# Two streams of TensorE products alternated in the half tiles of a mixture of experts, and a step of VectorE's order moved in the attention in front of it

## The chip, the cores and the metric

One Trainium2 (trn2) chip, one of its cores. The metric is the device time of one execution in microseconds (us).
## The reference, cut to what matters

One layer on x of 8 x 512 tokens with 256 features:

```python
qkv = x @ w_qkv.T                      # 16 heads of 16
q, k = rope(rms_norm(q, qw), rms_norm(k, kw))
x = layernorm(x + (softmax(causal(q @ k.T / 4)) @ v) @ w_proj.T)
normed = x * rsqrt(mean(x * x) + 1e-8) * norm_weight
shared = relu(normed @ sw1 + sb1) @ sw2 + sb2          # 256 -> 1024 -> 256
w, idx = top_2(sigmoid(normed @ router_w.T))           # of 8 experts, weights normalised
routed = sum over the two of w * (relu(normed @ ew1[e] + eb1[e]) @ ew2[e] + eb2[e])
out = layernorm(x + shared + routed)
```

The kernel keeps fp32 accuracy by splitting each operand into a high and a low fp16 half and adding three products (high x high, high x low, low x high).

## The kernel before

**Front stage.** The attention of the eight blocks c (512 tokens each), the routing, and the scatter of token rows to the experts are one software pipeline. All engines go through positions g = -33 to 209; `due(offsets, g)` lists the jobs of a kind at a position: block c does a job with offset o at g = 20c + o. So a block takes 20 positions, and several blocks are in work at once. At one position an engine does its kinds of jobs in a fixed order that its `step(g)` spells out. What this case touches, by position within a block (modulo 20):

- Position 18: TensorE transposes the last query and key rows of block c + 2 (`TR`, L1511 for the queries, L1517 for the keys). ScalarE copies the query columns (L886), VectorE the key columns (L1301), both into `stk`. TensorE's first score product of the next block (`UNITS`, p = 0, L1470, position 0) waits for both copies.
- Position 18 too: `added(c, 1)` on VectorE (L1111 to L1123) adds the projection to x and takes mean and variance; GpSimd's `norms` (L648 to L658) and `shifted` (L678) follow at position 19 from its result `vv`.
- Positions 17 and 1: `normalised(c, 0)` and `normalised(c, 1)` on VectorE, for the pairs of row tiles 0 and 1 of block c: two products `xnf` (L1133), the high half (L1136) and the low half (L1137) of the token rows `xnh`. They wait for GpSimd's `x1_done`. Their readers are TensorE's transposes at offsets 42 and 48 (positions 2 and 8) and GpSimd's scatters from offset 58 on.
- Positions 0 to 8, VectorE: normalised queries and keys (`qn`), GpSimd's copies of them (L631, L638, L639) and its half of the rotation (L619, L622), `averaged` at positions 4, 6, 8 and 10 (L1092, L1093; output `an`), which frees the bank `mb` that TensorE's L1622 fills.
- At some positions VectorE also makes the low half of a chunk of expert weights (L1335); at position 17 this comes behind everything else of that position.

**Expert stage.** Tokens sorted by expert form N_ROUTED = 39 tiles: tiles 0 to 31 have 256 rows, tiles 32 to 38 have 128 rows ("half tiles"). Ten tiles of the shared expert (256 rows) follow. Each tile has a first layer, `hidden`: 8 chunks hc x 6 products, whose stationary operand is a 128 x 128 block of the weights and whose moving operand is the tile's rows (256 or 128 columns); and a second layer, `output`: per 128 rows, 8 chunks x 3 products, whose moving operand is 256 columns of weights.
```python
def step(h, par, i):
    if i is None or i + 2 <= R_LAST:
        turn_rows(h + 1, par)                  # transposes of tile i + 2
    hidden(h + par, 1 - par, i == R_LAST)      # first layer of tile i + 1
    output(h, par)                             # second layer of tile i
```

Behind the first layer of a tile, ScalarE applies bias and ReLU (L950) and makes the high half (L955), in two halves of four chunks; VectorE makes the low half (L1351, semaphore `h_lo`, two counts per tile), then VectorE evicts the tile before (L1363). Each tile's ReLU waits until the low half of the tile before is made (`hf` has one buffer). `output` waits for both counts of `h_lo` of its tile.

Of the kernel before, what the change touches and what calls it, by code (L numbers as in the profile page):

```python
# [16 lines left out]
P = 128  # L17
NB, T, D = 8, 512, 256
NH, HD = 16, 16
NT = T // P  # L20
DC = D // P
# [15 lines left out]
TT = 256  # L37
# [47 lines left out]
AT = (32, 36)  # L85
PROJ = (34, 38)
NORMS = (35, 39)
XN_ROWS = (37, 41)
XN = (42, 48)
LG = (52,)  # L90
WEIGH = (54,)
# [30 lines left out]
def due(offsets, g):  # L122

    return [((g - off) // NPOS, i) for i, off in enumerate(offsets)
            if (g - off) % NPOS == 0 and 0 <= (g - off) // NPOS < NB]
# [2 lines left out]
CHUNKS = tuple(range(4 * LATE_E)) + tuple(range(4 * NE, N_CHUNKS))  # L128
N_RAW = N_CHUNKS - len(CHUNKS)
assert CHUNK_AT + (len(CHUNKS) - 1) * CHUNK_GAP <= EARLY_IN - 7 and len(CHUNKS) % 2 == 0  # L130

def chunk_due(g):
# [46 lines left out]
def rows_of(h, par):  # L180

    return P if isinstance(h, int) and N_FULL <= 2 * h + par < N_ROUTED else TT
# [32 lines left out]
def program(nc, a, S, keep):  # L215
# [86 lines left out]
    with ExitStack() as ctx:  # L302
# [90 lines left out]
        def routed_tiles(eng, step):  # L393

            step(0, 0, 0)
            step(0, 1, 1)
            with eng.Fori(1, LOOP_END // 2) as h:
                step(h, 0, None)
                step(h, 1, None)
            for i in range(LOOP_END, R_LAST + 1):  # L400
                step(i // 2, i % 2, i)

        with nc.Block() as block:
# [595 lines left out]
            def _(dve):  # L999
# [286 lines left out]
                def step(g):  # L1286
# [30 lines left out]
                        summed(c, t)  # L1317
                    for c, t in due(ROPE, g):
                        rope(c, t)
                    for c, u in due(XN_ROWS, g):  # L1320
                        normalised(c, u)
                    for c, _ in due(LG, g):
                        chosen(c)
# [123 lines left out]
            def _(pe):  # L1447
# [228 lines left out]
                def weights(e, chunk, w, col, n):  # L1676

                    if e is None:
                        return wts_s[:, chunk * 2 * CH + w * CH + col:chunk * 2 * CH + w * CH + col + n]
                    return wts[:, bass.ds(e * EW + (chunk * 2 * CH + w * CH + col), n)]  # L1680

                def hidden(h, par, late=False):

                    i = h * 2 + par
                    size = rows_of(h, par)
                    if late:
                        e = None
                        pe.wait_ge(S(f"x_in{par}"), (h - first(par) + N_EARLY // 2 + 1) * 16)
                    else:
                        e = pe.value_load(tab[0:1, 0, bass.ds(i, 1)], min_val=0, max_val=NE - 1)  # L1690
                        pe.wait_ge(S("experts_in"), (e + 1) * 16)
                        pe.wait_ge(S("xgT_ready"), i + 1)
                    for hc in range(HC):
                        if hc % 2 == 0:
                            pe.wait_ge(S("relu_done"), (N_EARLY + i - 1) * HC + hc + 2)
                        n = 0
                        for c in range(DC):
                            for x, w in PIECES:
                                last = pe.matmul(hb[hc // 2][:, (hc % 2) * TT:(hc % 2) * TT + size],  # L1699
                                                 weights(e, c, w, hc * P, P), xgT[:, par, x * DC + c, 0:size],  # L1700
                                                 start=(n == 0), stop=(n == 5))
                                n += 1
                        if hc % 2:
                            last.then_inc(S("h_done"), 1)

                def output(h, par, late=False):
                    i = h * 2 + par
                    e = None if late else pe.value_load(tab[0:1, 0, bass.ds(i, 1)], min_val=0, max_val=NE - 1)  # L1708
                    pe.wait_ge(S("h_lo"), (N_EARLY + i + 1) * 2)
                    pe.wait_ge(S("y_ready"), N_EARLY + i - 1)  # L1710
                    for j in range(rows_of(h, par) // P):
                        n = 0
                        for hc in range(HC):
                            for x, w in PIECES:
                                last = pe.matmul(ybank[par][:, j * D:(j + 1) * D],  # L1715
                                                 hh[:, par, x, hc, P * j:P * j + P],
                                                 weights(e, DC + hc * D // CH, w, hc * D % CH, D),
                                                 start=(n == 0), stop=(n == 3 * HC - 1))
                                n += 1
                    last.then_inc(S("y_done"), 1)  # L1720

                hidden(0, 0)

                def step(h, par, i):
                    if i is None or i + 2 <= R_LAST:
                        turn_rows(h + 1, par)
                    hidden(h + par, 1 - par, i == R_LAST)
                    output(h, par)

                routed_tiles(pe, step)  # L1730
                hidden(first(0), 0, True)
                output(first(1), 1, True)
                with pe.Fori(first(0), N_TILES // 2) as h:
                    hidden(h, 1, True)
                    output(h, 0, True)
                    hidden(h + 1, 0, True)
                    output(h, 1, True)
                output(N_TILES // 2, 0, True)

assert (LOOP_END - 4) % 8 == 0 and N_ROUTED % 2 == 1 and N_LATE % 2 == 0
# [58 lines left out]
```

## Time and profile before

| | |
|---|---|
| time, three runs | 1005.59, 1008.41, 1010.66 us (median 1008.41) |
| the profiled execution | 1011.32 us, span 1009.6 us |
| front stage up to the last scores | to about 394 us |
| early shared tiles, routing table, first gathers | to about 486 us |
| routed tiles of 256 rows | 486 to 842 us |
| routed half tiles | 842 to 890 us |
| shared tiles and the end | 890 to 1009.6 us |

A row of a timeline has the start in us, the length, the engine, the line of the kernel, the operation with out<-in, the count, and in brackets the idle time of the engine before it and what ended that. PEld is TensorE's weight load, PEldq its queue's register work. "issue" is time in which an engine waited for nothing that the profile shows.

### The profile page before, as it was taken

What the parts mean: (1) busy time and instruction counts of PE and PEld (TensorE: products, weight loads), DVE (VectorE), ACT (ScalarE), POOL (GpSimd) and SP (SyncE); (2) the same over time, 40 slices, a digit from 0 to 9 for tenths busy, and PEclk for the clock granted to TensorE, in tenths of its full rate; (3) what the DMA queues carried; (4) which work ended last, traced back from release to release, by engine and by line L of the source; (5) the groups of instructions that cost most, each with busy time, mean ns of one, the idle gap of its engine ahead of it and who ended that gap; (6) DMA issues with size and microseconds to landing.
All of it is one profiled execution on the core that took longest, in us unless ns stands there. A gap on an engine that the chain in (4) does not pass through costs nothing.

```text
span 1009.6 us, 26459 instructions
## 1 busy us (share of the span) xinstructions
PE 918.6 (91%) x9048; PEld 697.4 (69%) x9049; DVE 603.6 (60%) x1185; ACT 622.9 (62%) x1023; POOL 436.4 (43%) x637
## 2 busy tenths in 40 slices
PE   3688998898888898889899999999999999999995
PEld 1344554454444555778788898898898887788884
DVE  6757888788978754766235444544433332228874
ACT  3598887787778786534446556645644544456753
POOL 4654666767676664465024233333313323212211
PEclk9899999899989999999999999999999999999998
DMA  6023232433323236476883121121211121147651
GB/s 207 22 64 105 78 112 85 150 104 127 105 86 106 106 122 217 164 274 203 282 269 99 45 71 51 64 74 47 69 53 64 61 72 54 44 124 246 209 156 42
DMA packets 69539, 116.98 MB, mean 116 GB/s; under 512 B 7792, under 2 KB 45808, under 8 KB 69328
## 3 DMA queue, kind: packets, MB, share of 16 engines
q1 hardware_dynamic: 52080, 81.51, 24.5%
q10 hardware_dynamic: 10896, 16.40, 5.5%
q0 software_dynamic: 6480, 17.97, 4.9%
q8 instruction: 51, 0.84, 0.3%
q14 instruction: 32, 0.26, 0.1%
HBM read 68.67 MB, written 47.18 MB: 115 GB/s over the span
## 4 chain that ended last, share of the span: by engine, by line
PE 61%; POOL 11%; DVE 10%; ACT 7%; issue 6%; DMA 4%; ACTq 0%; SPq 0%; POOLq 0%; DVEq 0%
PE hb L1699 23%; PE yb L1715 23%; PE pv_bank L1492 5%; DMA xg_rows<-xnh,sl_i 3%; ACT prob L796 2%; PE ma L1501 2%; POOL nat L631 2%; POOL xg_rows L669 2%; PE slot L1470 2%; PE tr L1574 2%; PE yb L1591 1%; PE slot L1479 1%; POOL nat L638 1%; POOL rsum L619 1%; POOL rsum L622 1%
## 5 line engine op out<-in xcount | busy, mean ns | idle before, releaser
L950 ACT ACTIVATE hf<-hb,b 128x256 f32<-128x256 f32 (+1 forms) x392 | 155.7, 453 | 233.7 <-PE hb L1699 214.6
L1351 DVE TENSOR_TENSOR hh<-hf,hh 128x1024 f16<-128x1024 f32 (+1 forms) x98 | 119.1, 1216 | 148.3 <-ACT hh L955 148.3
L1699 PE MATMUL hb<-xgT,wts 128*128 128x256 f16 (+1 forms) x1872 | 202.1, 264 | 0.9 <-ACT hf L950 0.4
L1715 PE MATMUL yb<-wts,hh 128*128 x1704 | 192.8, 273 | 4.4 <-DVE hh L1351 4.4
L724 POOL DMA_INDIRECT y_tok<-yb,dest x71 | 73.7, 1038 | 276.6 <-DVE yb L1363 259.1
L1699 PEld LDWEIGHTS hb<-xgT,wts 128*128 x1872 | 171.7, 98 | 24.1 <-issue 2.3
L796 ACT ACTIVATE prob<-slot 128x1024 f32<-128x1024 f32 x160 | 162.3, 1046 | 39.4 <-PE slot L1479 38.8
L1715 PEld LDWEIGHTS yb<-wts,hh 128*128 128x128 f16 x1704 | 165.7, 98 | 25.5 <-issue 5.7
L955 ACT ACTIVATE hh<-hf 128x1024 f16<-128x1024 f32 (+1 forms) x98 | 97.6, 996 | 3.1
L1501 PE MATMUL ma<-wqkv,xTh 128*128 128x512 f16 (+1 forms) x384 | 78.9, 353 | 17.1 <-DVE xTh L1020 10.1
L1363 DVE SCALAR_TENSOR_TENSOR yb<-yb,b2bc 128x512 f32<-128x512 f32 (+1 forms) x39 | 25.1, 644 | 104.0 <-PE yb L1715 101.0
L1470 PE MATMUL slot<-stk 64*128 64x128 f16 (+3 forms) x512 | 63.5, 307 | 26.0 <-ACT prob L796 11.1
L1492 PE MATMUL pv_bank<-prob,vst 128*32 128x512 f32 (+3 forms) x1024 | 81.0, 460 | 1.1 <-ACT prob L796 1.1
L669 POOL DMA_INDIRECT xg_rows<-xnh,sl_i x64 | 74.0, 1157 | 17.9 <-POOL xnh L667 17.4
L1501 PEld LDWEIGHTS ma<-wqkv,xTh 128*128 128x128 f16 x384 | 37.4, 102 | 42.7 <-issue 24.7
L1492 PEld LDWEIGHTS pv_bank<-prob,vst 128*32 128x32 f32 x1024 | 31.4, 115 | 49.6 <-issue 42.9
L1479 PE MATMUL slot<-mask_b,ident_b 128*128 128x256 bf16 (+1 forms) x320 | 56.7, 260 | 0.0
L1470 PEld LDWEIGHTS slot<-stk 64*128 64x128 f16 x512 | 17.4, 94 | 55.8 <-issue 28.2
L1699 PE MATMUL hb<-xgT,wts_s 128*128 128x256 f16 x480 | 54.0, 273 | 0.0
L1715 PE MATMUL yb<-wts_s,hh 128*128 128x256 f16 x480 | 53.9, 273 | 0.0
L1699 PEld LDWEIGHTS hb<-xgT,wts_s 128*128 128x128 f16 x480 | 46.9, 98 | 5.5
L1715 PEld LDWEIGHTS yb<-wts_s,hh 128*128 128x128 f16 x480 | 46.9, 98 | 5.5
(197 smaller groups left out, 1430.8 us busy)
## 6 DMA issues: line engine op xcount, KB each, us to landing
wts<-in_w_all SPq DMA_DIRECT2D x19, 512.0 KB, 5.1
stage<-in_w_all SPq DMA_DIRECT2D x16, 512.0 KB, 4.5
w_split<-chunk_hl SPq DMA_DIRECT2D x16, 512.0 KB, 2.9
wts<-y_tok SPq DMA_DIRECT2D x32, 256.0 KB, 4.4
xg<-xg_rows ACTq DMA_DIRECT2D x30, 264.0 KB, 2.7
wts<-w_split SPq DMA_DIRECT2D x3, 2048.0 KB, 9.1
xTf<-in_xT SPq DMA_DIRECT2D x8, 512.0 KB, 3.8
xin<-in_x SPq DMA_DIRECT2D x8, 512.0 KB, 4.0
```

What stands on the lines that cost most here:

```text
L669: pool.indirect_dma_start(a["xg_rows"], bass.IndirectOffsetOnAxis(ap=sl_i[:, c % 2, t, k:k + 1], axis=0), xnh[:, c % 2, t, :], None).then_ ...
L724: pool.indirect_dma_start(a["y_tok"], bass.IndirectOffsetOnAxis(ap=dest[:, slot, j:j + 1], axis=0), yb[:, par, j, :], None).then_inc(S(f"y ...
L796: act.activation(dst, src, ACT.Exp, scale=ATT_SCALE).then_inc(S("exp_done"), 1)
L950: act.activation(hf[:, c, 0:size], hb[c // 2][:, (c % 2) * TT:(c % 2) * TT + size], ACT.Relu, bias=bias, scale=1.0 / WS).then_inc(S("relu_ ...
L955: act.activation(hh[:, par, 0, cs, 0:size], hf[:, cs, 0:size], ACT.Copy).then_inc(S("h_hi"), 1)
L1351: dve.tensor_tensor(hh[:, par, 1, cs, 0:size], hf[:, cs, 0:size], hh[:, par, 0, cs, 0:size], ALU.subtract).then_inc(S("h_lo"), 1)
L1470: pe.matmul(slot[:, 512 * x + col:512 * x + col + T - P * j], stk[rows, par, 1, pr, P * j:P * j + P], stk[rows, par, 0, pr, P * j:T], star ...
L1479: last = pe.matmul(out, ident_b[:], mask_b[:, 0:diag[0], :], start=False, stop=True, skip_group_check=True)
L1492: last = pe.matmul(pv_bank[32 * r:32 * r + 32, P * j:T], vst[:, c % 2, j, 4 * g + r, :], prob[:, g % 2, r, SEG[j]:SEG[j] + T - P * j], sta ...
L1501: last = pe.matmul(out, xTh[:, c % 2, x, k, P * t:P * t + P], wqkv[:, y, k, cols], start=(n == 0), stop=(n == len(pieces) - 1))
L1699: last = pe.matmul(hb[hc // 2][:, (hc % 2) * TT:(hc % 2) * TT + size], weights(e, c, w, hc * P, P), xgT[:, par, x * DC + c, 0:size], start ...
L1715: last = pe.matmul(ybank[par][:, j * D:(j + 1) * D], hh[:, par, x, hc, P * j:P * j + P], weights(e, DC + hc * D // CH, w, hc * D % CH, D), ...
```

## The change

The second and the first layer of the half tiles are issued in turn: in the steps i = 31 to 37 each first-layer product of tile i + 1 is followed by its share of the second-layer products of tile i: one each in step 31 (48 and 48), one after every second in steps 32 to 37 (48 and 24). The expert's number of a tile is read once there and kept for its second layer. In all steps `output` waits for the first count of `h_lo` at its start and for the second one before its thirteenth product. And `XN_ROWS` goes from (37, 41) to (38, 43) for the blocks 0 to 6; at position 18 VectorE's order puts it behind the key columns' copy and behind `added`. The last block keeps (37, 41).

```diff
-XN_ROWS = (37, 41)
+XN_ROWS = (38, 43)
+XN_ROWS_LAST = (37, 41)
...
+def rows_due(g):
+
+    return due(XN_ROWS, g) if g < NPOS * (NB - 1) + XN_ROWS_LAST[0] else [
+        (NB - 1, u) for u, off in enumerate(XN_ROWS_LAST) if NPOS * (NB - 1) + off == g]
...
-                    for c, u in due(XN_ROWS, g):
+                    for c, u in rows_due(g):
                         normalised(c, u)
...
+                def output_product(h, par, e, k):
+
+                    i = h * 2 + par
+                    j, n = divmod(k, HC * len(PIECES))
+                    hc, (x, w) = n // len(PIECES), PIECES[n % len(PIECES)]
+                    if k == 0:
+                        pe.wait_ge(S("h_lo"), (N_EARLY + i) * 2 + 1)
+                        pe.wait_ge(S("y_ready"), N_EARLY + i - 1)
+                    if j == 0 and n == HC // 2 * len(PIECES):
+                        pe.wait_ge(S("h_lo"), (N_EARLY + i + 1) * 2)
+                    ins = pe.matmul(ybank[par][:, j * D:(j + 1) * D], hh[:, par, x, hc, P * j:P * j + P],
...
+                def both(i, e_in, e_out):
+
+                    pe.wait_ge(S("experts_in"), (e_in + 1) * 16)
+                    pe.wait_ge(S("xgT_ready"), i + 2)
+                    n_out = rows_of(i // 2, i % 2) // P * HC * len(PIECES)
+                    for k in range(N_IN):
+                        hidden_product((i + 1) // 2, (i + 1) % 2, e_in, k)
+                        for m in range(k * n_out // N_IN, (k + 1) * n_out // N_IN):
+                            output_product(i // 2, i % 2, e_out, m)
...
                 def step(h, par, i):
                     if i is None or i + 2 <= R_LAST:
                         turn_rows(h + 1, par)
-                    hidden(h + par, 1 - par, i == R_LAST)
-                    output(h, par)
-
+                    if i is None or i < N_FULL - 1:
+                        hidden(h + par, 1 - par)
+                        output(h, par, expert_of(h * 2 + par))
+                        return
+                    e_out = expert[0] if expert else expert_of(i)
+                    if i < R_LAST:
+                        expert[:] = [expert_of(i + 1)]
+                        both(i, expert[0], e_out)
+                    else:
+                        hidden(h + par, 1 - par, True)
+                        output(h, par, e_out)
```

`hidden_product(h, par, e, k)` and `output_product` issue one product each of what `hidden` and `output` issued in their loops, with the waits at the same products but for `h_lo`.

## Rows read from the trace of the kernel before

**Rows 1.** The page: busy time of TensorE and VectorE over the span.

```profile
PE 918.6 (91%) x9048; PEld 697.4 (69%) x9049; DVE 603.6 (60%) x1185; ACT 622.9 (62%) x1023; POOL 436.4 (43%) x637
```

**Rows 2.** Windows: length, busy us of each engine, granted clock, DMA share, GB/s.

```profile
216.00:222.00 6.00, 4.93 (x50) 2.01 (x50) 5.56 (x15) 5.14 (x9) 2.97 (x7) 1.00 0.10 37
250.00:300.00 50.00, 42.43 (x404) 22.58 (x405) 42.73 (x94) 35.25 (x49) 33.56 (x53) 0.90 0.30 102
266.50:270.20 3.70, 3.70 (x16) 1.09 (x14) 3.46 (x13) 1.99 (x3) 2.00 (x4) 0.55 0.99 290
```

**Rows 3.** Timeline of TensorE: first scores of blocks 3 to 7.

```profile
167.36 0.39 PE L1470 MATMUL slot<-stk 64*128 64x512 f16 x2 [2.69 <-issue]
...
217.07 0.39 PE L1470 MATMUL slot<-stk 64*128 64x512 f16 x2 [1.91 <-issue]
...
266.20 0.39 PE L1470 MATMUL slot<-stk 64*128 64x512 f16 x2 [3.72 <-DVE stk L1301]
...
316.15 0.39 PE L1470 MATMUL slot<-stk 64*128 64x512 f16 x2 [2.11 <-issue]
...
359.74 0.39 PE L1470 MATMUL slot<-stk 64*128 64x512 f16 x2 [0.40 <-ACT stk L886]
```

**Rows 4.** Timeline of ScalarE: query columns' copy ahead of blocks 3 and 6.

```profile
164.18 1.08 ACT L886 ACTIVATE stk<-ma 128x1024 f16<-128x1024 f16 x1
...
313.55 1.08 ACT L886 ACTIVATE stk<-ma 128x1024 f16<-128x1024 f16 x1
```

**Rows 5.** Timeline of VectorE ahead of block 5, positions 17 and 18.

```profile
261.05 1.55 DVE L1133 SCALAR_TENSOR_TENSOR xnf<-y,vv,ffn_nw 128x256 f32<-128x256 f32 x2
...
264.27 1.23 DVE L1335 SCALAR_TENSOR_TENSOR chunk_hl<-stage,chunk_hl 128x1024 f16<-128x1024 f32 x1
265.41 0.68 DVE L1301 COPY stk<-mc 128x1024 f16<-128x1024 f16 x1
```

**Rows 6.** Timeline of TensorE: the same six products behind two block starts.

```profile
217.51 1.46 PE L1501 MATMUL ma<-wqkv,xTh 128*128 128x512 f16 x6
...
266.64 2.56 PE L1501 MATMUL ma<-wqkv,xTh 128*128 128x512 f16 x6
```

**Rows 7.** Waits (sum, times, longest): two of 200 to 400 us, the last of the whole span.

```profile
POOL vv L648 <- DVE vv L1121: 39.8, 10, 8.8
...
DVE xnf L1133 <- POOL y L678: 9.1, 4, 3.3
...
PE mb L1622 <- DVE an L1093: 11.5, 7, 2.6
```

**Rows 8.** Timeline of TensorE: step 36, first layer of step 37, first shared tile.

```profile
874.50 4.32 PE L1699 MATMUL hb<-xgT,wts 128*128 128x128 f16 x48
879.43 2.81 PE L1715 MATMUL yb<-wts,hh 128*128 x24 [0.61 <-DVE hh L1351]
...
882.45 4.38 PE L1699 MATMUL hb<-xgT,wts 128*128 128x128 f16 x48 [0.21 <-issue]
...
890.12 5.40 PE L1699 MATMUL hb<-xgT,wts_s 128*128 128x256 f16 x48
```

**Rows 9.** TensorE's queue by line, step 36: median ns, first and last start.

```profile
L1690 PEldq TENSOR_LOAD <-keep_tab x1: 298/298/298, 873.5 to 873.5; - x1
...
L1699 PEldq FUSED_REGOPS  x32: 46/46/46, 874.4 to 878.4; - x32
...
L1708 PEldq TENSOR_LOAD <-keep_tab x1: 305/305/305, 878.6 to 878.6; - x1
...
L1715 PEldq FUSED_REGOPS  x16: 46/46/60, 879.3 to 881.4; - x16
```

**Rows 10.** The chain in order of time: a full second layer; first products of tile 32.

```profile
510.82 5.24 PE yb L1715 x48
...
832.97 0.68 PE hb L1699 x12
```

**Rows 11.** Timeline of VectorE: the second low half of tile 37 (step 36).

```profile
880.28 0.69 DVE L1351 TENSOR_TENSOR hh<-hf,hh 128x512 f16<-128x512 f32 x1 [1.36 <-ACT hh L955]
```

## What the change is expected to do

> **What bounds the kernel now.** I read first the page's busy times [rows 1]: TensorE works in 91% of the span, VectorE in 60%. So TensorE's idle time and its slow stretches are what can be won; VectorE matters only where somebody waits for it. Then the windows [rows 2]: in a typical 50 us of the front stage (a block's period is about 49 us by the block starts [rows 3]) TensorE works 42.4 us and VectorE 42.7 us, both close to full, with a mean granted clock of 0.90.
>
> Then TensorE's timeline, for its gaps. In the front stage the largest ones stand ahead of the first scores of a block [rows 3]: 2.69, 1.91, 3.72, 2.11 and 0.40 us for blocks 3 to 7, 10.8 us together. VectorE's timeline says why [rows 5]: ahead of block 5 it makes the token rows (261.05 to 264.27, 3.2 us), then a chunk's low half, and only then, from 265.41 to 266.09, the key columns' copy; the scores start at 266.20. Where the profile names "issue" instead, the copy ends just ahead of the scores as well.
>
> In the expert stage the array is full in the tiles of 256 rows (48 products in 5.24 us, 109 ns each [rows 10]) and not in the half tiles. Step 36 goes from 874.50 (start of its first layer) to 882.45 (start of the next), 7.95 us [rows 8]. Its products alone would need less: 12 first-layer products ran in 0.68 us [rows 10], 57 ns each, when enough of them were queued, so 48 of them 2.7 us, and 24 of the second layer 2.6 us, together 5.3. The queue's rows show what sets the pace [rows 9]: 32 register instructions for the first layer, started from 874.4 to 878.4, 129 ns apart; a read of the table at 878.6; then 16 more from 879.3 to 881.4, 140 ns apart with the first longer one. Two reads and 48 register instructions fill the 7.9 us without a hole. So the half tiles are bound by TensorE's queue. The 0.6 us idle ahead of the second layer, which the profile puts down to VectorE's low half [rows 8], is the table read between 878.6 and 879.3: the low half that this second layer needs is the one of the tile before, made a step earlier.
>
> **The change part by part. A: the half tiles.** The same products and, I take it, the same 48 register instructions per step are issued. In steps 32 to 37 one of the two table reads goes: from 878.6 to 879.3 [rows 9], 0.7 us. 6 x 0.7 = 4.2 us. In step 31 both reads stay. Its array work is 48 x 57 + 48 x 109 ns = 7.97 us, and register instructions for it (32 for the first layer, 16 for the second, as their addresses are kept for the second 128 rows) need 48 x 0.13 = 6.2 plus two reads: about as long, so I count nothing for the queue there. At the end of step 37 the array is behind the queue by the part in which 24 second-layer products (2.62 us) take longer than their register instructions (2.1 us); alternated, a second-layer product stands between two short ones and nothing piles up: 0.5 to 0.7, say 0.7 us. Sum of A: 4.9 us less.
>
> The bounds of A. Register instructions may cost less when they are spread: then the array decides, 5.3 + 0.2 us (four transposes) per step instead of 8.0: 6 x 2.5 + 0.7 in step 31 = 16 us less. Or a first-layer product among second-layer ones goes at their 109 ns: 72 x 0.109 + 0.9 (a read with what follows it, 873.5 to 874.4) + 0.2 = 8.9 per step, 6 us more in six steps, and 1 more in step 31. I stay near the queue's own rows, as they are the nearest: 7.3 us per step (0.9 + 48 x 0.13 + waits).
>
> TensorE's page of the Trainium skill (TensorE: Matmul & The Clock Gate, section "Back-to-back issue gap") puts pairs of a weight load and a product of 128 columns at about 81 ns each however they are queued. The rows show 57 ns in a full queue and 90 ns in the half tiles (4.32 us for 48), so it is not the array's own pace here; by the page's figure a step would be 48 x 0.081 + 2.6 + 0.2 = 6.7 us if its pairs were the bound, and A 7.8 us instead of 4.2 for the six steps (an estimate from that page).
>
> New waits. The second layer of tile i now starts one product behind the start of tile i + 1's first layer. Its first half is safe: made in the middle of the step before. The second half is needed by the thirteenth product, behind 24 first-layer and 12 second-layer products with their 24 register instructions: 0.9 + 24 x 0.13 = 4.0 us into the step. It is ready at 880.97, 2.2 us behind the last first-layer product (874.50 + 4.32 = 878.8) [rows 8, 11]. That covers it with 1.8 us to spare; if this cover is gone, each us costs seven, one per step. Queued behind that wait are all later products of both tiles, and behind them ScalarE. The eviction of a tile comes behind the low half of the next on VectorE, 2.2 us later than now, and GpSimd's scatter behind it; the two output banks give it a whole step. In all other tiles the second wait comes at a product for which both halves have long been made: nothing.
>
> **B: the rows behind the copy.** At position 18 VectorE now does the copy first. What then holds the scores is ScalarE's copy of the query columns; the four of blocks 3 to 6 end at 165.26, 215.75, 264.00 and 314.63 (the first and the last are shown [rows 4]). With 0.1 us to the start, blocks 3 to 6 can start 2.0, 1.2, 2.1 and 1.4 us earlier [rows 3, 4], 6.7 us together. For block 5 VectorE still makes the chunk's low half first (1.2 us from 261.05), and its copy would end at 262.9, ahead of ScalarE's. For block 7, with 0.40 us already put down to ScalarE's copy [rows 3], and block 2 I count nothing. Block 5's and block 3's long gaps have a price of their own: behind 3.72 us idle the granted clock is 0.55 in 266.5 to 270.2, where it is 1.00 behind the 1.91 us of block 4 [rows 2], and six products take 2.56 us instead of 1.46 [rows 6]. With gaps below 1.6 us I expect the full clock: 1.1 us each, 2.2.
>
> Does it last? The moved rows (3.2 us for one pair [rows 5]) are still made, by a VectorE that is nearly full. But they leave the path from the projection over `vv` to GpSimd, which waits 39.8 us for `vv` in 200 us [rows 7]: GpSimd's norms start up to 3 us earlier, and with them its copies and rotations that VectorE waits for later in the block. At position 3 the second pair falls ahead of `averaged`, for which TensorE waits 11.5 us in all [rows 7]; what VectorE saves at position 1 (its wait for GpSimd's rows, 9.1 us in four times there [rows 7]) pays for most of it. So I let the 6.7 + 2.2 = 8.9 us stand. Bounds of B: nothing, if VectorE's own work sets the period (42.7 of 50 us are near it), to 5 starts x 3.2 us = 16 plus 3 for the clock = 19 less, if the chain over GpSimd is the only one.
>
> **Sum.** 4.9 + 8.9 = 13.8 us off. The profiled execution took 1011.3 us, 2.9 more than the median of 1008.4; the differences are taken from the latter: 994.6 us.
>
> **The rivals.**
> 1. Only A holds: VectorE is the bound of the front stage, and the later pair at position 3 eats what the copy gives. 1008.4 - 4.9 = 1003.5. For it: VectorE's 42.7 us of 50. Against: its waits of up to 3.3 us for GpSimd [rows 7]. Chance 0.13.
> 2. Only B holds: register instructions get dearer when two experts' addresses are alternated (more of them, or waits between them), and eat the 4.9. 999.5. Chance 0.12.
> 3. More than I count: the chain over GpSimd shortens by 3.2 us per block (1008.4 - 4.9 - 19 = 984.5), or the array's own pace decides in the half tiles (1008.4 - 16 - 8.9 = 983.5). Chance 0.15. By the Trainium skill's pair figure above the time would be 1008.4 - 7.8 - 0.7 - 8.9 = 991.0 (an estimate), within my likeliest case's range.
> 4. Slower: the pair at position 3 (3.2 us [rows 5]) comes ahead of `averaged` just where TensorE already waits for `an`; TensorE idles longer, its clock falls, and a stretch behind it costs another 1.1 us [rows 6]. 6 blocks x 4.3 us = 26, less 4.9 of A and with B's gain gone: 1008.4 + 26 - 4.9 = about 1029; from 0.8 us per block on it ends above the kernel before. It decides if VectorE reaches position 4 later than today. Against: it is freed of a wait at position 1. Chance 0.05.
>
> **How the numbers follow.** The likeliest case, both parts at their rows, has 0.55 and its own range is 989 to 1000. Rivals 1 and 2 lie at 1003.5 and 999.5, the larger gains down to 983. A range of 984 to 1004 leaves out the slow rival, the very ends and part of rival 1. Half a per cent, about what a measurement of this kernel can tell from no change, is 5 us: faster is below 1003.4. The likeliest case, rivals 2 and 3 and a sixth of rival 1 lie there: 0.55 + 0.12 + 0.15 + 0.02 = 0.84. Within: the rest of rival 1, 0.11. Slower: rival 4, 0.05.
>
> **What would show it.** In the profile after: first scores of blocks 3 to 6 with less than 1 us of idle time ahead of them, named after ScalarE's copy; the first scores of block 7 some 9 us earlier than 359.74; granted clock 1.00 behind the starts of blocks 3 and 5; steps 32 to 37 of 7.2 to 7.4 us with 48 register instructions each and no idle ahead of L1715's line; the first shared tile's first layer at about 876 instead of 890.12. What would make it wrong: more register instructions per step than 48, a wait for VectorE's low half inside the alternated stretch, waits for `an` that grow by as much as the block starts shrink, or a new stretch at the low clock.

## The result, and the profile after

| | before | after |
|---|---|---|
| median | 1008.5 us (1005.59 to 1010.99, 6 runs) | 999.8 us (993.53 to 1002.31, 6 runs) |
| profiled execution, span | 1011.32, 1009.6 us | 1000.01, 998.3 us |
| ratio, 95% interval | | 0.9888 (0.9859 to 0.9917) |

The kernel became 8.7 us faster by the medians and 11.3 us by the spans; 13.8 were predicted (994.6 us, range 984 to 1004). Run once more beside other kernels, the changed kernel had a ratio of 0.9866 (0.9831 to 0.9902).

In the changed kernel the lines have moved: scores L1480, products for the next block L1511, ScalarE's copy L896, VectorE's copy L1311, the rows L1143 to L1147, `an` L1103, first layer L1705, second layer L1721, table read L1694, transposes of a routed tile L1584. The first page row, against [rows 1]:

```profile
PE 911.2 (91%) x9048; PEld 694.1 (70%) x9049; DVE 600.1 (60%) x1185; ACT 624.2 (63%) x1023; POOL 433.5 (43%) x637
```

TensorE is busy 7.4 us less with the same 9048 products: the same work, with less time at the low clock and in the half tiles. The windows, in the columns of [rows 2]:

```profile
125.00:355.00 230.00, 209.62 (x2321) 119.34 (x2320) 202.43 (x472) 191.29 (x263) 163.35 (x249) 0.99 0.34 112
250.00:300.00 50.00, 45.11 (x496) 25.34 (x498) 44.15 (x103) 41.71 (x57) 36.04 (x55) 1.00 0.30 97
```

From 250 to 300 us the granted clock is 1.00 where it was 0.90; over 125 to 355 us it is 0.99, where the kernel before had 0.95 with TensorE busy for 204.76 us and 2204 products. The first scores of blocks 3 to 7 (TensorE's timeline), against [rows 3]:

```profile
168.70 0.39 PE L1480 MATMUL slot<-stk 64*128 64x512 f16 x2 [0.65 <-ACT stk L896]
...
214.71 0.39 PE L1480 MATMUL slot<-stk 64*128 64x512 f16 x2 [0.65 <-ACT stk L896]
...
262.45 0.39 PE L1480 MATMUL slot<-stk 64*128 64x512 f16 x2 [1.59 <-ACT stk L896]
...
307.56 0.39 PE L1480 MATMUL slot<-stk 64*128 64x512 f16 x2 [0.33 <-ACT stk L896]
...
350.10 0.39 PE L1480 MATMUL slot<-stk 64*128 64x512 f16 x2
```

3.22 us idle instead of 10.83, and what ends it is ScalarE's copy. The same stretch as a whole, from the first scores of block 2 to those of block 7, holds 2268 products in both kernels; here it is before, after, and in the kernel "second pair only" of the experiments:

```profile
122.72:359.74 237.02, 211.39 (x2268) 118.42 (x2269) 200.07 (x461) 186.84 (x257) 160.36 (x242) 0.95 0.32 107
...
126.09:350.10 224.01, 204.87 (x2268) 117.26 (x2269) 197.19 (x460) 186.16 (x257) 160.06 (x242) 0.98 0.34 112
...
120.99:358.05 237.06, 208.31 (x2269) 117.34 (x2270) 200.51 (x461) 187.84 (x257) 159.43 (x242) 0.97 0.31 107
```

Of the 13.0 us, TensorE's idle time has 6.5 (25.6 to 19.1) and its busy time for the same products the other 6.5 (211.4 to 204.9). VectorE's order ahead of block 5 shows why the starts have moved, against [rows 5]: the chunk's low half, the copy, and the token rows only behind `added`:

```profile
259.34 1.22 DVE L1345 SCALAR_TENSOR_TENSOR chunk_hl<-stage,chunk_hl 128x1024 f16<-128x1024 f32 x1
260.47 0.68 DVE L1311 COPY stk<-mc 128x1024 f16<-128x1024 f16 x1
261.07 0.68 DVE L1121 SCALAR_TENSOR_TENSOR y<-mb,xin 128x512 f32<-128x512 f32 x1
...
263.66 0.88 DVE L1143 SCALAR_TENSOR_TENSOR xnf<-y,vv,ffn_nw 128x256 f32<-128x256 f32 x2
```

The half tiles are read off the four transposes that open each of the steps 31 to 36:

```profile
826.73 0.39 PE L1584 MATMUL tr<-keep_ident,xg 128*128 128x128 f16 x4
835.39 0.39 PE L1584 MATMUL tr<-keep_ident,xg 128*128 128x128 f16 x4
841.71 0.39 PE L1584 MATMUL tr<-keep_ident,xg 128*128 128x128 f16 x4
849.15 0.39 PE L1584 MATMUL tr<-keep_ident,xg 128*128 128x128 f16 x4
856.62 0.39 PE L1584 MATMUL tr<-keep_ident,xg 128*128 128x128 f16 x4
864.05 0.39 PE L1584 MATMUL tr<-keep_ident,xg 128*128 128x128 f16 x4
864.98 0.35 PE L1705 MATMUL hb<-xgT,wts 128*128 128x128 f16 x2 [0.54 <-ACT hf L960]
...
878.79 5.40 PE L1705 MATMUL hb<-xgT,wts_s 128*128 128x256 f16 x48
```

Before, they stood at 832.59, 842.46, 849.72, 857.78, 865.93 and 873.98:

```profile
832.59 0.39 PE L1574 MATMUL tr<-keep_ident,xg 128*128 128x128 f16 x4
```

Step 31 takes 8.66 us instead of 9.87 and step 32 takes 6.32 instead of 7.26. The steps 33 to 35 take 7.43 to 7.47, 7.45 on the mean, instead of 8.1. From the opening of step 31 to the first shared tile it is 52.1 us now, 57.5 before (832.59 to 890.12 [rows 8]). The queue's rows of step 36, against [rows 9]: 32 + 16 register instructions, and one table read per step (the second of the two listed, at 871.3, is the next step's):

```profile
L1705 PEldq FUSED_REGOPS  x32: 46/46/46, 864.9 to 871.2; - x32
L1721 PEldq FUSED_REGOPS  x16: 46/46/46, 865.2 to 871.1; - x16
L1694 PEldq TENSOR_LOAD <-keep_tab x2: 300/302/303, 864.0 to 871.3; - x2
```

The 0.54 us idle ahead of 864.98, named after ScalarE, lie inside the read (from 864.0 to the first register instruction at 864.9): it is the read.

Not all of the front stage's lead survives. Block 7 starts 9.6 us earlier than before although block 2 started 3.4 us later (126.09 against 122.72), so B had won 13.0 us by then. At the opening of step 31 the lead is 5.9 us, 9.2 counted from block 2. Part of the loss is seen at 398 us (the second pair of lines is from before):

```profile
398.30 1.09 PE L1632 MATMUL mb<-ident_f,raw 128*128 128x128 f32 x4 [4.75 <-DVE an L1103]
399.19 3.72 PE L1564 MATMUL hb<-xgT,wts_s 128*128 128x256 f16 x24
...
405.16 0.63 PE L1622 MATMUL mb<-ident_f,raw 128*128 128x128 f32 x4 [2.64 <-DVE an L1093]
405.63 2.78 PE L1554 MATMUL hb<-xgT,wts_s 128*128 128x256 f16 x24
```

Here the lead has fallen from 9.6 to 6.9 us, but some of it comes back: the first product of the first routed tile stands 8.0 us earlier than before (478.18 against 486.19). The rest is lost behind it, in part where TensorE waits for the token rows that the DMA gathers, 3.01 us at 486.59 where it was 1.89 at 493.49:

```profile
486.59 1.03 PE L1584 MATMUL tr<-keep_ident,xg 128*128 128x128 f16 x8 [3.01 <-DMA xg<-xg_rows]
...
493.49 0.62 PE L1574 MATMUL tr<-keep_ident,xg 128*128 128x128 f16 x8 [1.89 <-DMA xg<-xg_rows]
```

For the wait at 398 us, VectorE's timeline names what is ahead of `an`: the first early tile's low half (position 163, L1271), and then block 6's second pair, which now falls at 163 instead of 161:

```profile
394.20 1.23 DVE L1271 TENSOR_TENSOR hh<-hf,hh 128x1024 f16<-128x1024 f32 x1 [6.96 <-issue]
395.35 0.88 DVE L1143 SCALAR_TENSOR_TENSOR xnf<-y,vv,ffn_nw 128x256 f32<-128x256 f32 x2
396.25 0.43 DVE L1146 CAST xnh<-xnf 128x512 f16<-128x512 f32 x1
396.71 0.69 DVE L1147 TENSOR_TENSOR xnh<-xnf,xnh 128x512 f16<-128x512 f32 x1
397.44 0.26 DVE L1102 RECIPROCAL rcp<-mb 128x16 f32<-128x16 f32 x1
397.73 0.42 DVE L1103 TENSOR_TENSOR an<-mb,rcp 128x256 f32<-128x256 f32 x1
```

### The profile page after: what moved, and what is told of

Same layout as the page of the kernel before. It is cut to its first block, busy times and chain, and to the rows that moved or that the text cites. A ratio compares the mean times of both kernels' runs of the same rounds, so it can differ in the third digit from the quotient of the medians.

```text
span 998.3 us, 26472 instructions
## 1 busy us (share of the span) xinstructions
PE 911.2 (91%) x9048; PEld 694.1 (70%) x9049; DVE 600.1 (60%) x1185; ACT 624.2 (63%) x1023; POOL 433.5 (43%) x637
## 4 chain that ended last, share of the span: by engine, by line
PE 59%; POOL 14%; DVE 9%; issue 7%; ACT 5%; DMA 4%; ACTq 0%; SPq 0%; POOLq 0%; DVEq 0%
PE hb L1705 24%; PE yb L1721 23%; DMA xg_rows<-xnh,sl_i 3%; PE pv_bank L1502 3%; POOL xg_rows L679 3%; POOL nat L641 2%; PE ma L1511 2%; ACT prob L806 2%; PE tr L1584 2%; POOL rsum L632 1%; PE slot L1480 1%; POOL nat L648 1%; POOL nat L649 1%; POOL rsum L629 1%; POOL y L688 1%
## 5 line engine op out<-in xcount | busy, mean ns | idle before, releaser
L960 ACT ACTIVATE hf<-hb,b 128x256 f32<-128x256 f32 (+1 forms) x392 | 154.7, 456 | 228.0 <-PE hb L1705 224.2
L1705 PE MATMUL hb<-xgT,wts 128*128 128x256 f16 (+1 forms) x1872 | 219.8, 264 | 2.6 <-ACT hf L960 2.1
L1721 PE MATMUL yb<-wts,hh 128*128 x1704 | 215.3, 273 | 0.1
L1705 PEld LDWEIGHTS hb<-xgT,wts 128*128 x1872 | 178.3, 98 | 25.3 <-issue 3.9
L1721 PEld LDWEIGHTS yb<-wts,hh 128*128 128x128 f16 x1704 | 166.5, 98 | 21.8 <-issue 0.6
L1511 PE MATMUL ma<-wqkv,xTh 128*128 128x512 f16 (+1 forms) x384 | 79.7, 356 | 17.4 <-DVE xTh L1030 10.3
L1480 PE MATMUL slot<-stk 64*128 64x128 f16 (+3 forms) x512 | 63.5, 306 | 19.3 <-ACT prob L806 9.4
L1502 PE MATMUL pv_bank<-prob,vst 128*32 128x512 f32 (+3 forms) x1024 | 76.5, 440 | 1.1 <-ACT prob L806 1.1
L1511 PEld LDWEIGHTS ma<-wqkv,xTh 128*128 128x128 f16 x384 | 38.4, 105 | 43.3 <-issue 24.1
L1705 PE MATMUL hb<-xgT,wts_s 128*128 128x256 f16 x480 | 54.0, 273 | 0.0
L1721 PE MATMUL yb<-wts_s,hh 128*128 128x256 f16 x480 | 53.9, 273 | 0.0
L1480 PEld LDWEIGHTS slot<-stk 64*128 64x128 f16 x512 | 17.2, 94 | 48.6 <-issue 21.0
L1721 PEld LDWEIGHTS yb<-wts_s,hh 128*128 128x128 f16 x480 | 47.0, 98 | 5.4
L1705 PEld LDWEIGHTS hb<-xgT,wts_s 128*128 128x128 f16 x480 | 47.0, 98 | 5.4
```

The lines of the kernel that those rows point to most:

```text
L960: act.activation(hf[:, c, 0:size], hb[c // 2][:, (c % 2) * TT:(c % 2) * TT + size], ACT.Relu, bias=bias, scale=1.0 / WS).then_inc(S("relu_ ...
L1480: pe.matmul(slot[:, 512 * x + col:512 * x + col + T - P * j], stk[rows, par, 1, pr, P * j:P * j + P], stk[rows, par, 0, pr, P * j:T], star ...
L1502: last = pe.matmul(pv_bank[32 * r:32 * r + 32, P * j:T], vst[:, c % 2, j, 4 * g + r, :], prob[:, g % 2, r, SEG[j]:SEG[j] + T - P * j], sta ...
L1511: last = pe.matmul(out, xTh[:, c % 2, x, k, P * t:P * t + P], wqkv[:, y, k, cols], start=(n == 0), stop=(n == len(pieces) - 1))
L1705: ins = pe.matmul(hb[hc // 2][:, (hc % 2) * TT:(hc % 2) * TT + size], weights(e, c, w, hc * P, P), xgT[:, par, x * DC + c, 0:size], start= ...
L1721: ins = pe.matmul(ybank[par][:, j * D:(j + 1) * D], hh[:, par, x, hc, P * j:P * j + P], weights(e, DC + hc * D // CH, w, hc * D % CH, D), ...
```

## The experiments

Each kernel was run beside the kernel before; ratios are to that, with 95% intervals. Since the intervals are 0.4 to 0.7% wide, the mechanisms are read from stretches of the profiled executions. "Block 2 at" is the time of its first scores; the columns behind it are the us between rows of TensorE's timeline, from one trace of each kernel: the first scores of block 2, those of block 7, the transposes that open steps 28 and 31, the first layer of the first shared tile.

| kernel | ratio | block 2 at | 2 to 7 | 7 to step 28 | steps 28 to 30 | step 31 to shared |
|---|---|---|---|---|---|---|
| before | 1 | 122.7 | 237.0 | 440.3 | 32.6 | 57.5 |
| changed | 0.9888 (0.9859 to 0.9917) | 126.1 | 224.0 | 444.1 | 32.6 | 52.1 |
| changed, again | 0.9866 (0.9831 to 0.9902) | 125.7 | 224.0 | 446.0 | 32.6 | 52.3 |
| A only | 0.9959 (0.9939 to 0.9978) | 125.0 | 237.2 | 439.6 | 32.6 | 52.3 |
| B only | 0.9897 (0.9868 to 0.9926) | 123.0 | 224.2 | 445.5 | 32.6 | 57.5 |
| block 6's pair back | 0.9833 (0.9802 to 0.9864) | 124.0 | 223.9 | 441.8 | 32.6 | 52.3 |
| two reads | 0.9882 (0.9854 to 0.991) | 124.9 | 224.0 | 443.7 | 32.6 | 56.8 |
| one read, in blocks | 0.9871 (0.9845 to 0.9898) | 125.4 | 224.2 | 445.0 | 32.6 | 53.2 |
| reads ahead | 0.9863 (0.9837 to 0.9889) | 124.2 | 223.9 | 442.6 | 36.2 | 47.6 |
| first pair only | 0.987 (0.9833 to 0.9907) | 122.7 | 227.6 | 438.6 | 32.6 | 52.1 |
| second pair only | 0.9999 (0.9975 to 1.0024) | 121.0 | 237.1 | 440.3 | 32.6 | 52.1 |
| first pair, reads ahead | 0.9857 (0.9824 to 0.989) | 121.0 | 228.2 | 445.4 | 36.3 | 47.6 |
| fixed addresses | 0.9778 (0.9747 to 0.9808) | 124.3 | 224.6 | 445.4 | 32.6 | 42.4 |
| second pair at 45 | 0.9893 (0.986 to 0.9925) | 121.1 | 224.6 | 445.0 | 32.6 | 52.4 |

**Each part alone.**

```diff
 # A only: the changed kernel with
-XN_ROWS = (38, 43)
+XN_ROWS = (37, 41)
 # B only: the kernel before with the new XN_ROWS, XN_ROWS_LAST and rows_due
```

> Part A alone: the changed kernel with both pairs of token rows back at offsets 37 and 41. My theory (the two parts add up, A is worth 5.4 us in the trace): 5 us less than the kernel before (ratio 0.995), the stretch from the last transposes to the first shared tile 52.1 us as in the changed kernel, the last scores of block 7 near 393.9 us as before. Rival (the parts are not independent: A is worth its 5.4 us only because other work arrives earlier): less than 3 us gained. Rival (nearly all of the 11 us is A's, and the front stage only shifted by chance): ratio 0.99.

> Part B alone: the kernel before with only the new places of the token rows. My theory: 5.5 to 6 us less than the kernel before (ratio 0.9945): 9 us gained up to the last scores of block 7 (at about 385), of which about 3 are lost again at about 398 us, behind the second pair of block 6. Rival (the front stage moved by accident, by other windows of the half clock): the block starts still have their gaps of 1.9 to 3.7 us, or the last scores lie within 2 us of 393.9.

The parts add up: 237.2 and 52.3 us for A only, 224.2 and 57.5 for B only, the values of the kernels that do or don't have the part. By the ratios A is worth 4.1 us and B 10.4, of about 1010; together 14.5, where the two comparisons of the changed kernel gave 11.3 and 13.5. B's gain exceeded what I expected of it (5.5 to 6 us), since that was taken from a single pair of traces in which block 2 happened to start 3.4 us late.

**The pair that falls behind the early tile.**

```diff
+ROWS_AT = {(c, u): NPOS * c + (XN_ROWS if c < NB - 1 and (c, u) != (NB - 2, 1) else XN_ROWS_LAST)[u]
+           for c in range(NB) for u in range(2)}
```

> The changed kernel with one job moved back: the second pair of rows of block 6 at offset 41 (position 161) instead of 43 (position 163), so ahead of the low half of the first early tile on VectorE. My theory (this pair behind that low half makes TensorE wait 4.75 us for `an` at 398 us and lose the clock behind it): 3 us less than the changed kernel (ratio to the kernel before 0.986), the wait for `an` there 2.6 us or less, and the 24 products of L1564 behind it in 2.8 us instead of 3.7. Rival (block 7's chain sets the end of the front stage, and the wait for `an` is where its lead is bound to end): no change against the changed kernel, 0.989, the wait only goes to another place.

The long wait goes as expected, from 4.75 to 2.65 us. But the 24 products behind it, which were expected to speed up from 3.72 to 2.8 us, take 4.45, at the low clock:

```profile
393.59 0.63 PE L1632 MATMUL mb<-ident_f,raw 128*128 128x128 f32 x4 [2.65 <-DVE an L1103]
394.06 4.45 PE L1564 MATMUL hb<-xgT,wts_s 128*128 128x256 f16 x24
```

From block 7 to step 28 it is 441.8 us, against 442.6 to 446.0 (mean 444.6) in the seven traces of kernels with offsets 38 and 43 in all blocks: 2.8 us less than their mean, near the 3 expected. That the missing wait brought this is not shown, for two reasons. The first routed tile starts 128.9 us behind block 7, no earlier than in the seven (128.1 to 131.1); what is gained is gained behind it, where the gathers are waited for. And the kernel "second pair only" has the long wait too, 4.68 us at 405.32, and takes 440.3 us, no more than the kernel before. The expectation's rival, that the wait only goes to another place, is not ruled out. The ratio of this kernel is the lowest of those that compute the whole layer; the intervals of this and of the changed kernel overlap, and they were not run beside each other.

**One read or two, alternated or not.**

```diff
 # two reads: in the half-tile steps
-                    e_out = expert[0] if expert else expert_of(i)
+                    e_out = expert_of(i)
 # one read, in blocks: in both()
                     for k in range(N_IN):
                         hidden_product((i + 1) // 2, (i + 1) % 2, e_in, k)
-                        for m in range(k * n_out // N_IN, (k + 1) * n_out // N_IN):
-                            output_product(i // 2, i % 2, e_out, m)
+                    for m in range(n_out):
+                        output_product(i // 2, i % 2, e_out, m)
```

> The changed kernel with the table read a second time in each half-tile step, for the second layer's expert, as the kernel before does; the products still alternate. My theory (TensorE's queue sets the pace and the read that is left out is the gain): 6 x 0.65 to 0.75, so 4 to 4.5 us more than the changed kernel (ratio 0.993), steps 32 to 37 of 8.1 us instead of 7.45. Rival (the alternation itself gives the gain, the read lies in the shade of the array): within 1 us of the changed kernel.

> The changed kernel with one table read per half-tile step, as in the change, but the products of the two layers issued in two blocks (all 48 first-layer products, then all 24 of the second), as in the kernel before. The stretch of the half tiles (first first-layer product of tile 32 to that of the first shared tile) took 57.3 us before, 51.8 after, 56.5 with alternation and two reads. My theory (the read is most of the gain, the alternation hides the array's lag at the end): 52.5 to 53 us, some 5 us off the kernel before together with nothing lost in the front stage, ratio 0.989. Rival (alternation is needed for the gain, because only then do waits and reads lie under products): 56 us or more.

The second read costs 56.8 - 52.1 = 4.7 us (7.45 to 8.1 per step): it is the gain. Alternation without it leaves 57.5 - 56.8 = 0.7. In blocks, with one read, the stretch is 53.2; the steps 33 to 35 take 7.36, 7.46 and 7.32 us, as fast as alternated ones. The difference of 1.1 lies in step 31, which opens at 827.06 and ends at 836.93 (9.87 us, as before), where the alternated one took 8.66. So in this kernel the alternation is worth 0.7 to 1.1 us and the read 4.3 to 4.7. Both prices are read from one trace of each kernel. The times do not show them: two reads has a ratio of 0.9882, like the changed kernel (0.9888 and 0.9866), where 0.993 was expected, and that lies above its interval (to 0.991). Why its times do not show the 4.7 us is open; part A as a whole does show in the times, as the 0.9959 of A only.

**No read in the half tiles.**

```diff
+                AHEAD = {28: (31, 32), 29: (33, 34, 35), 30: (36, 37, 38)}
+                    if i in AHEAD:
+                        expert.update({m: expert_of(m) for m in AHEAD[i]})
-                    e_out = expert[0] if expert else expert_of(i)
+                    e_out = expert[i]
-                        both(i, expert[0], e_out)
+                        both(i, expert[i + 1], e_out)
```

> The changed kernel with the table reads of tiles 31 to 38 all made in the steps of tiles 28 to 30, where the array has 10.5 us of work per step and the queue about 7.6, and kept in registers. Steps 32 to 37 then hold 48 register instructions and waits, no read. My theory (the queue still sets the pace there): 6.7 to 6.8 us per step instead of 7.45, 7 x 0.65 = 4.5 us less over the half tiles (stretch 47.3 us instead of 51.8), nothing lost in steps 28 to 30; ratio 0.984. Rival (the queue's work of steps 28 to 30 becomes longer than the array's): those steps grow by what the half tiles gain. Rival (a value kept in a register is read back at a cost): more than 48 register instructions per step, no gain.

The theory and its first rival both hold: the half tiles take 47.6 us (4.5 less, as expected, in steps of 6.8), and the steps 28 to 30 take 3.7 us more. Their transposes:

```profile
790.63 0.61 PE L1584 MATMUL tr<-keep_ident,xg 128*128 128x128 f16 x8
802.47 0.61 PE L1584 MATMUL tr<-keep_ident,xg 128*128 128x128 f16 x8
814.88 0.39 PE L1584 MATMUL tr<-keep_ident,xg 128*128 128x128 f16 x4
826.85 0.39 PE L1584 MATMUL tr<-keep_ident,xg 128*128 128x128 f16 x4
```

11.84, 12.41 and 11.97 us, where the others have 10.93, 10.93 and 10.70: two reads add 0.9, three 1.5 and 1.3. At 0.65 us a read, 0.4 to 0.7 us of a group is hidden and the rest is not. My 7.6 us of queue work against 10.5 of the array suggested a slack of 3 us that the queue cannot use: it does not run that far ahead of the array. In step 28 the first of the reads starts at 789.6, 1.0 us before the array opens the step at 790.63, and the array then stands idle for 0.58 us; in step 29, with one read more, for 1.20. One read per step, apart from the others, was not tried.

**How fast the array could go.**

```diff
-                        hidden_product((i + 1) // 2, (i + 1) % 2, e_in, k)
+                        hidden_product((i + 1) // 2, (i + 1) % 2, 0, k)
-                            output_product(i // 2, i % 2, e_out, m)
+                            output_product(i // 2, i % 2, 0, m)
```

> The changed kernel, in whose steps 31 to 37 the weights of both layers are always those of expert 0, at addresses known beforehand (so it leaves out the choice of the expert there; the table is still read and waited on). No register instruction is left between the products. My theory (the register instructions set the pace of the half tiles, not the array): the step falls from 7.45 us to the array's 5.3 us plus one read and the transposes, about 6.2 us, the stretch from 51.8 to about 44 us, ratio some 0.98. Rival 1 (a product of 128 columns between two of 256 cannot go at 57 ns, but at 80 or more): 7 us per step, stretch 49 us. Rival 2 (the chain over ScalarE's ReLU and VectorE's low half sets the step): no change, 51.8 us.

The stretch falls to 42.4 us, the steps 32 to 35 to 5.5, 6.1, 5.7 and 5.5. Three products, two of 128 columns and one of 256, start every 0.22 us, the 57 + 57 + 109 ns of [rows 10]:

```profile
853.02 0.28 PE L1705 MATMUL hb<-xgT,wts 128*128 128x128 f16 x2
853.13 0.27 PE L1721 MATMUL yb<-wts,hh 128*128 128x256 f16 x1
853.24 0.28 PE L1705 MATMUL hb<-xgT,wts 128*128 128x128 f16 x2
853.36 0.27 PE L1721 MATMUL yb<-wts,hh 128*128 128x256 f16 x1
...
858.82 0.28 PE L1721 MATMUL yb<-wts,hh 128*128 128x256 f16 x1 [0.44 <-DVE hh L1361]
```

So the register instructions set the pace of the changed kernel's half tiles: 9.6 us of its 52.1 are theirs. The last line shows what is late next, by 0.44 us: VectorE's low half, for which the prediction counted 1.8 us to spare in steps of 7.3.

**Which of the two pairs, and where.**

```diff
 # first pair only
-XN_ROWS = (38, 43)
+XN_ROWS = (38, 41)
 # second pair only: (37, 43)     second pair at 45: (38, 45)
```

> The changed kernel with only the first pair of rows moved (offsets 38 and 41). The first pair lay at offset 37 (position 17), between the projection and the key columns' copy. My theory: the block starts (blocks 3 to 6) lose their gaps as in the changed kernel, since the second pair (position 1) lies behind them anyway; the last scores near 386 us, so ratio 0.989 or better, and no wait of 4.75 us for `an` near 398 us. Rival (both moves are needed, as the second pair then falls on GpSimd's late rows): half of the front stage's gain, 0.993.

> The changed kernel with only the second pair of rows moved (offsets 37 and 43). My theory: the block starts keep their gaps of 1.9 to 3.7 us behind VectorE's key copy, last scores at 394 to 398 us as before; time that of part A alone, ratio 0.996. Rival (the gain of the front stage comes from VectorE no longer waiting for GpSimd's rows at position 1, 9.1 us in four waits before): the last scores come 4 us or more earlier.

> The changed kernel with the second pair of rows two positions later still (offsets 38 and 45), behind `averaged` of position 4 and ahead of that of position 6. With 41 the stretch from block 2's first scores to block 7's took 228.6 us, with 43 it took 225.0, before 237.0. My theory (the place of the second pair moves only a little work between waits for `an`): 223 to 229 us, last scores near 386, and again 2 us or more lost behind them; ratio 0.985 to 0.99. Rival (the slow rival of the prediction: later rows push `averaged` back, TensorE waits for `an` and its clock falls): 232 us or more, ratio 0.993 or above.

The first pair alone brings 9.4 of the 13.0 us between blocks 2 and 7; the second alone none (its block starts keep 3.12, 2.60, 3.73 and 2.10 us of idle), but 3.6 more on top of the first. The ratio of the second alone is a miss: 0.9999, where 0.996 was expected, that of A only, though its trace has A's 5.4 us in the half tiles. Its twelve times go from 1003.6 to 1015.5 us (median 1011.6), and the profiled execution, at 1004.2, is the third fastest of them; in which stretch the others were slower stays open. Behind block 7 both moves together lose 4.5 us against the mean of 440.1 of the three traces in which the first pair stands at 37, the first pair alone less in one trace (438.6). The other trace of that kind, with the reads ahead, has 445.4, so this is not settled. With the first pair only there is, as expected, no wait of 4.75 us near 398 us: it is 2.65 us at 396.01, again with 24 products in 4.45 us behind it. At offset 45 the stretch is much the same (224.6 us), and so is the loss: the slow rival, in which later rows push `averaged` back in each block, was not met even two positions on.

**A better version, and the change again.** It joins the edit of reads ahead with that of the first pair only.

> A version meant to beat both kernels: part A with the table reads of tiles 31 to 38 made ahead in the steps of tiles 28 to 30, and of part B only the first pair of rows (offset 38; the second stays at 41). My theory: the half tiles in 47.4 us (57.3 before), the front stage up to the first routed tile at 475 to 478 us (486 before); 14 to 19 us less than the kernel before, ratio 0.981 to 0.986, and 3 to 5 us less than the changed kernel run beside it. Rival (the steps of tiles 28 to 30 pay for the reads): no less than the changed kernel.

> The changed kernel itself once more, on the chip of its neighbours. By the traces the parts are worth 5.4 us (half tiles) and about 9 us (front stage, block 2 to the first routed tile), so 14 us, where the first comparison gave 0.9888 (0.9859 to 0.9917), 11 us. My theory (the first comparison fell on the low side): ratio 0.985 to 0.988. Rival (something that the stretches do not show takes 3 us back): 0.989 or above again.

997.3 and 999.1 us, ratios 0.9857 and 0.9866: no difference that these runs can tell, where 3 to 5 us were expected. The reads made ahead give back 3.7 of their 4.5 us, and what leaving the second pair in place saves behind block 7 is no more than these traces scatter. No version was shown to beat the changed kernel; block 6's pair put back is the candidate.

## Why the prediction came out as it did

- **A, 4.9 us.** Measured 5.4 in the stretch, 5.2 between A only and before. The read term (6 x 0.7) holds: 4.3 to 4.7. The step was to be 7.3 us and is 7.45; the 48 register instructions, the cover of the low half and the idle-free second layer came as said. Two small terms came out the other way round: step 31, counted at nothing, gives 1.2 us (9.87 to 8.66), because it had 48 short products waiting on the queue and then 48 long ones waiting on the array, and alternated each hides the other. The 0.7 us at the end of step 37 are hardly there: from the opening of step 36 to the shared tile it is 14.74 us against 16.14, 1.4 less, which is the two reads.
- **A's bounds.** The lower one, 16 us if the array decides, is near what the fixed addresses showed (57.5 to 42.4 us, 15.1 less), but only with the register instructions left out. The upper one (a short product at 109 ns among long ones) was not met. By the Trainium skill (TensorE: Matmul & The Clock Gate, section "Back-to-back issue gap") the pairs would have needed about 81 ns; the section gives that figure for a sustained stream of such pairs, and "however they are queued" was the prediction's own addition. The run with fixed addresses does not agree with the figure: its short products start 57 ns apart even between long ones.
- **B's starts, 6.7 us.** Measured 7.2 in the four starts that the term speaks of (10.43 to 3.22 us idle); block 7's, counted at nothing, gives 0.4 more. Blocks 3, 4 and 6 start with less than 1 us of idle, block 5 with 1.59: its wait for ScalarE's copy was longer than I allowed.
- **B's clock, 2.2 us.** This term was mis-sized. B won 13.0 us up to block 7. The idle time of TensorE there fell by 6.5 us (the starts' 7.6, less 1.1 by which other waits grew), and the busy time for the same 2268 products by 6.5, where 2.2 were counted. I priced only the stretches right behind two starts. The kernel before also ran at 1.2 GHz later in the same blocks (192 to 198 and 291 to 297 us have a granted clock of 0.50 in its trace, behind waits of 1.9 us for `an`); a mean of 0.95 is some 23 of 230 us at that level. In the trace after two short stretches are left, at 186 and at 326 us. That the shorter gaps are what brought this was not tested by itself. Nor does the granted clock alone set the length of this stretch: with only the second pair moved TensorE was busy 3.1 us less than before, at 0.97 instead of 0.95, and idle 3.1 us more, and the stretch stayed at 237.1 us. GpSimd waited less for `vv` too (29.5 us from 200 to 400 us, 39.8 before), as the prediction's third rival has it; no run separates what this chain gave from what the clock gave.
- **For the last blocks, nothing.** This step failed. The stretch from block 7 to step 28 has 4.5 us more in the mean of the seven traces with offsets 38 and 43. Waits for `an` that grow were named as what would make the prediction wrong. One grew to 4.75 us, where the early tile's low half stands between the pair and `averaged`; between blocks 2 and 7 they grew a little as well, from 7.6 us to 8.9 in the changed kernel's trace and 10.4 in its second one. The long wait is not shown to be what the 4.5 us are: the kernel with only the second pair moved has it and loses nothing (440.3 us). Part of the spread lies in tiles whose instructions the change does not touch: from the first routed product to step 28 the traces take 312.9 to 316.6 us, A only 316.4. Why the last blocks lose stays open.
- **The sum.** B is worth 677.2 - 668.7 = 8.5 us from block 2 to step 28 (means of three traces with the first pair at 37 and of seven with 38 and 43 throughout); 8.9 were predicted. That they agree is luck: the clock term was too small, and the loss in the last blocks was missing. With A's 5.4 it is 13.9 us, against 13.8. Yet the two comparisons gave 11.3 and 13.5 us of about 1010. Part of it lies ahead of block 2, which started at 123.0 to 126.1 us (mean 124.7) in the eight traces with 38 and 43 and at 121.0 to 125.0 (mean 122.3) in the other six. The only moved work ahead of that start is block 0's first pair, and it is moved in three of the other six as well, whose block 2 starts at 121.0 to 122.7. So what sets the eight apart from them, the place of the second pair, comes behind block 2's start, and the difference can't be its work. It arises earlier: in the trace after, TensorE is at the low clock at 46 and 67 us. It looks like chance from one execution to the next; no run tested this.
- **The rivals.** Only A: ruled out by B only. Only B: by A only. More than counted: up to block 7 B gave 13.0 us of this rival's 19, by the chain or by the clock, and the array's pace was not reached in the half tiles. Slower: not met.

## What to carry to other kernels

Where operand addresses come from registers, count the queue's instructions per product before the array's time: a read of a table on that queue costs its full length when the queue is the bound, and most of it in a group even where the array is. When a job is moved to a later position for all blocks, look at each block's neighbours at the new position, the last blocks first, because other work is interleaved there. Look at the granted clock over a whole stretch, not only right behind the gaps, and split the stretch into idle time and busy time of the same products: a higher clock is worth time only where the idle time does not grow by as much. And where single executions differ by 10 us, trust a gain of 5 us only if both its stretch and the times show it.

## What was not expected of the hardware

- With addresses known beforehand, products of 128 and 256 columns alternate at 57 and 109 ns, each at its own pace; with 48 register instructions for 72 products, at 103 ns on the mean (7.45 us).
- TensorE's queue hides little scalar work: in the reads made ahead, of a group of two or three table reads (0.65 us each) only 0.4 to 0.7 us was covered by products of 109 ns.
- A shorter gap does not secure the clock: behind 2.65 us of idle the next 24 products took 4.45 us instead of 2.78 in two kernels (393.59 and 396.01 us), where behind 4.75 us they took 3.72. Behind 2.64 us in the kernel before they took 2.78, the full clock.
